# Extra TensorE products without a reader at three kinds of waits in a decoder layer

## The reference

```python
x = x + _L0_attn_ref(_layernorm(x))
x = x + _L0_xattn_ref(_layernorm(x), ctx_512, Wq, Wkv_expand, Wout)
x = x + _L0_ffn_ref(_layernorm(x), w_gate, w_up, w_down)
```

## Time and profile before

| | us |
|---|---|
| three runs, median (lowest to highest) | 1776.98 (1774.51 to 1780.01) |
| the profiled execution's own time | 1770.3 |
| its span, first to last instruction | 1767.3 |
| PE busy | 1404.7 (79%) |
| DVE busy | 1141.0 (65%) |
| ACT busy | 857.7 (49%) |
| POOL busy | 547.8 (31%) |
| mean granted clock of TensorE | 0.926 |

### The profile page before, as it was taken

How to read it: one execution, slowest core, us unless ns; L and a number is a source line. 1 busy time by engine, 2 the same in 40 slices (tenths; PEclk the granted TensorE clock), 3 DMA queues, 4 the chain that set the end, 5 groups by cost and what they waited for, 6 DMA issues and landing times.

```text
span 1767.3 us, 30712 instructions
## 1 busy us (share of the span) xinstructions
PE 1404.7 (79%) x11035; PEld 815.5 (46%) x11104; DVE 1141.0 (65%) x2475; ACT 857.7 (49%) x2098; POOL 547.8 (31%) x494
## 2 busy tenths in 40 slices
PE   1224898889988898779988899779988899779977
PEld 0113554445544554445544554445544554445533
DVE  8993355864578455864578455864578456864576
ACT  2442364445634564455634564455635564455622
POOL 5872000650046200640046101640046101640045
PEclk9999899898989899998989899998989899998998
DMA  5311000000010000010010000010010001000001
GB/s 184 107 54 37 1 1 23 9 17 9 1 25 13 19 1 25 7 25 1 2 24 13 19 1 25 7 25 1 1 25 13 19 2 25 7 19 1 1 0 24
DMA packets 25283, 36.04 MB, mean 20 GB/s; under 512 B 2480, under 2 KB 10672, under 8 KB 25136
## 3 DMA queue, kind: packets, MB, share of 16 engines
q1 hardware_dynamic: 25136, 34.09, 7.3%
HBM read 25.69 MB, written 8.39 MB: 19 GB/s over the span
## 4 chain that ended last, share of the span: by engine, by line
PE 45%; DVE 25%; ACT 10%; issue 9%; POOL 2%; DMA 0%; SPq 0%; ACTq 0%; DVEq 0%; POOLq 0%
PE psum L1092 10%; PE psum L526 8%; PE psum L1109 7%; PE psum L1130 5%; DVE top L807 4%; DVE inter L833 3%; PE psum L1146 3%; PE psum L1169 3%; PE psum L1095 3%; PE psum L1191 2%; ACT silu L990 2%; DVE nmx L757 2%; DVE q L803 2%; DVE xn L508 2%; PE psum L1118 1%
## 5 line engine op out<-in xcount | busy, mean ns | idle before, releaser
L757 DVE TENSOR_REDUCE nmx<-psum 128x2 f32<-128x256 f32 (+3 forms) x256 | 211.0, 824 | 209.4 <-PE psum L1095 207.4
L503 POOL TENSOR_TENSOR rstd<-var_eps,minus_half 128x1 f32<-128x1 f32 x96 | 59.9, 624 | 867.3 <-DVE var_eps L497 867.1
L952 ACT ACTIVATE p<-psum,nmx 128x384 f32<-128x384 f32 (+3 forms) x512 | 265.9, 527 | 65.3 <-DVE nmx L757 58.8
L1092 PE MATMUL psum<-k_f,q_f 32*128 32x128 f32 (+3 forms) x1024 | 226.7, 520 | 11.7 <-ACT q_f L932 5.9
L770 DVE COPY pt<-psum 128x128 f32<-128x128 f32 (+3 forms) x256 | 124.6, 487 | 159.9 <-PE psum L1109 159.4
L1109 PE MATMUL psum<-ident,p 128*128 128x128 f32 x1280 | 205.2, 288 | 19.7 <-ACT pt L976 16.5
L691 POOL TENSOR_TENSOR inter<-inter,rscale 128x512 f32<-128x512 f32 x128 | 141.5, 1105 | 213.4 <-DVE rscale L841 212.8
L1191 PE MATMUL psum<-wd_sb,iq_t 128*128 128x512 bf16 x503 | 146.2, 416 | 46.2 <-DVE x_res L850 27.1
L976 ACT COPY pt<-psum 128x128 f32<-128x128 f32 (+3 forms) x256 | 109.1, 426 | 149.4 <-PE psum L1109 148.0
L1109 PEld LDWEIGHTS psum<-ident,p 128*128 128x128 f32 x1280 | 143.0, 145 | 54.4 <-ACT pt L976 24.8
L1169 PE MATMUL psum<-wg_sb,xq_t 128*128 128x512 bf16 x452 | 132.8, 415 | 39.4 <-ACT xq_t L983 29.9
(11 more groups left out here) (102 smaller groups left out, 2389.8 us busy)
## 6 DMA issues: line engine op xcount, KB each, us to landing
x_in<-in_x_dram SPq DMA_DIRECT2D x32, 256.0 KB, 4.0
out_dram<-x_res SPq DMA_DIRECT2D x64, 128.0 KB, 2.4
w_raw<-in_w_gate_dram SPq DMA_DIRECT2D x16, 256.0 KB, 2.7
w_raw<-in_w_up_dram SPq DMA_DIRECT2D x16, 256.0 KB, 3.0
w_raw<-in_w_down_dram SPq DMA_DIRECT2D x16, 256.0 KB, 3.8
ctx_in<-in_ctx_t_dram SPq DMA_DIRECT2D x8, 256.0 KB, 2.9
wq_raw<-in_wq_t_dram SPq DMA_DIRECT2D x1, 1024.0 KB, 8.1
wo_sb<-in_wo_t_dram SPq DMA_DIRECT2D x1, 1024.0 KB, 10.0
```

The lines of the kernel that those rows point to most:

```text
L757: dve.tensor_reduce(nmx2[:, u % UNITS, 2 * pr:2 * pr + 2], where(("scores2", oc, qt, pr))[:, :, 0:(qt + 1) * P], AX_X, ALU.max, negate=Tru ...
L952: ins = act.activation(p2[:, (4 * u + hh) % P2_RING, 0:m], where(label)[:, hh % 2, 0:m], ACT.Exp, bias=nmx2[:, u % UNITS, hh:hh + 1], accu ...
L1092: pe.matmul(where(label)[:, j, 0:m], q_f[rows, oc % 2, qt * P:(qt + 1) * P], k_f[rows, oc % 2, 0:m], start=True, stop=False)
```

## The change

A helper `keep_busy` waits until a PSUM slot is free and then issues a number of products into it: the bf16 identity is the stationary operand, 512 columns of `wd_sb` are the moving one, and the result has no reader; the label's own products overwrite it. It is called at four places, of three kinds: three products before a batch's first scores and four behind them (in the slot of the first transposed probabilities), four before each tile's first gate product, between the tile's transposes and the wait for ACT's copy, and seven before a batch's first quantised transposes of the inner result. In `gate_up` the wait for the slot is put ahead of the wait for the copy of `xq_t`.

```diff
@@ -1048,6 +1048,12 @@
             @block.tensor
             def _(pe):
 
+                def keep_busy(label, times):
+
+                    until_free(pe, label)
+                    for _ in range(times):
+                        pe.matmul(where(label)[:, 0, :], ident_b[:], wd_sb[:, 0, :], start=True, stop=True)
+
                 def project_q(oc):
                     out_cols = slice(oc % OC * P, (oc % OC + 1) * P)
                     until_free(pe, ("q", oc))
@@ -1161,9 +1167,10 @@
                 def gate_up(i):
                     t, m = divmod(i, 4)
                     label = ("gateup", i)
+                    until_free(pe, label)
                     if m == 0:
+                        keep_busy(label, 4)
                         until_freed(pe, ("xqT", t))
-                    until_free(pe, label)
                     for j, w in enumerate((wg_sb, wu_sb)):
                         for c in range(C):
                             last = pe.matmul(where(label)[:, j, :], xq_t[:, t % 2, c * P:(c + 1) * P],
@@ -1209,8 +1216,10 @@
                 for b in range(B):
 
                     first, end = b * UNITS, (b + 1) * UNITS
+                    keep_busy(("scores2", *units[first], 0), 3)
                     for pr in range(2):
                         score2(first, pr)
+                    keep_busy(("probsT2", *units[first], 0), 4)
                     for u in range(first, end):
                         oc, qt = units[u]
                         more = oc % OC + 1 < OC
@@ -1243,6 +1252,8 @@
                             gate_up(b * CHUNKS + i)
                         if INTER_LAG < i <= CHUNKS + INTER_LAG:
                             down(b * CHUNKS + i - INTER_LAG - 1)
+                        if i == INTER_LAG:
+                            keep_busy(("interT", b * CHUNKS), 7)
                         if INTER_LAG <= i < CHUNKS + INTER_LAG:
                             turn_inter(b * CHUNKS + i - INTER_LAG)
                         if b + 1 < B:
```

## The result

The changed kernel takes 1722.83 us (median of 4 runs, 1719.87 to 1724.87), the kernel before 1775.74 (4 runs, 1770.95 to 1780.01). The ratio is 0.970, with a 95% interval from 0.968 to 0.973. That is faster by 53 us; 1740 was forecast, with 1729 to 1750 around it. The profiled execution took 1723.65 us, with a span of 1721.9; between the two spans there are 45.4 us.

A forecast was written before the change was run, and what follows sets the result against it. TensorE at half clock behind each batch's first scores was taken as the bound. 35.0 there + 1.9 feed-forward - 0.4 added products = 36.5 us off 1770.3, 2.1%, giving 1740 us from the 1776.98 median; range 1729 to 1750, outer 1722 to 1760.

The forecast's parts named there:

- The mechanism: Behind each batch's first scores: short pauses precede the clock's fall; filling them holds 1.00 and gives 35.0 us.
- the marks: Each unit's closing transpose on L1118; foretold 4.8 and 7.95 us behind the first mark and the one after it.
- Rival 1: First scores: high clock holds in some batches only, each fall returns 4.5 us; four of eight give 1757; chance 0.12.
- Rival 2: Clock falls for another reason than the pauses, or products don't count; 0 to 3 us added, 1777 to 1780; chance 0.06.
- The first mark: First scores: stretch from 405.35 to the first unit's closing transpose, 1.77 us low, 0.97 high; 0.80 us gained a batch.
- the sum for the first groups: First group of heads, all eight batches: 8 x (0.80 + 2.16) + 2.27 + 4 x 1.4 + 3 x 1.15 = 35.0 us gained.
- The feed-forward part: First quantised transposes to next first scores: 4.7 us gained, 2.8 us paid back by low-level products, net 1.9 us.
- the 4.7 us expected for the fall: First quantised transposes: the fall goes, giving 0.9 us in batches 1, 3, 5 and about 1 in 0 and 7.
- One sign of being right: Feed-forward part: its length stays within 1 us of 92.5.
- The loss at the gate: First gate product: four products at low level take 1.71 us against at most 1.1; about 0.7 us late a tile.
- rival 3: Slower: low-level products on the path, at the gate 0.7 us a tile; 1783 to 1799, 1791 taken; chance 0.06.
- The lower bound of 1722: Whole kernel: range's low end, if scores give 40 and feed-forward 6 us and timed runs hold more low stretches.

The follow-up runs named there:

- the first experiment: Changed kernel with only the products before and behind the first scores (3 + 4), none at the gate or quantised transposes: 1726.60 us, ratio 0.975.

## Why the prediction was right, and where its sum was short

**The mechanism was right at the first scores.** The granted clock behind them is 1.00 in all eight batches; the marks are 4.78 and 7.96 us apart as foretold. The 64-column products and the seven placed early speak for work in the pauses behind the scores and against the rivals. Over all traces, 55 of the 56 first groups with four or eight full products behind the scores stay high throughout, and none of the 40 with no product there does. Of the seven added products only the four matter; the three before the scores, which the prediction counted as part of the remedy, do nothing. Rival 1 (it holds in some batches only) didn't happen in the changed kernel; with the same products at the scores it did in one batch of the first experiment. Rival 2 falls: the pauses are all shorter than a microsecond, and filling one of 0.73 us in each batch is worth some 40 us in all. The section of the Trainium skill (TensorE: Matmul & The Clock Gate, "Why this matters for your kernels") names only a long idle gap; taken as the only way to the low level, this does not agree with the traces here, and the measurement decides.

**The first mark was mis-sized.** "What lies between the fall and 405.35 I count at nothing" was wrong. Between the transpose at 403.67 and the scores at 405.35 stand three products of `project_k`; that takes 1.68 us before, and 396.78 - 395.83 = 0.95 after. The row that the sum left out, in the kernel before:

```profile
403.80 1.63 PE L526 MATMUL psum<-ctx_hl,wkv_hl 128*128 128x512 f32 x3
```

From the first scores to the first mark it was 8.44 us and is 6.98, 1.46 us a batch less and not 0.80: 5.3 us in eight batches. With this term the sum for the first groups is 40.3, and 40.2 was measured.

**The feed-forward part gave 4.7 us, not 1.9, and not where the sum had it.** The fall behind the first quantised transposes did go, and with it 1.4 us of the step from the first to the second tile in batches 1, 3 and 5. But these parts are no shorter: 93.4 us each before, 93.8, 93.2 and 93.2 after. From the fourth tile's transposes to the next scores they take 35.9 us instead of 34.8, with a low stretch of 6.8 us near the end (in batch 1 from 569.8) where 3.4 us were low before. Batch 1, first the kernel before, then the changed one, with the transposes of the second and fourth tile (the first tile's and the next scores of the kernel before are in the earlier trace rows, of the changed one in its rows here):

```profile
519.46 0.61 PE L1157 MATMUL psum<-ident_b,xq 128*128 128x128 bf16 x4
562.48 0.40 PE L1157 MATMUL psum<-ident_b,xq 128*128 128x128 bf16 x4 [0.73 <-ACT iq_t L998]
```

```profile
490.98 0.38 PE L1163 MATMUL psum<-ident_b,xq 128*128 128x128 bf16 x4 [0.20 <-POOL xq L691]
505.14 0.40 PE L1163 MATMUL psum<-ident_b,xq 128*128 128x128 bf16 x4
548.90 0.61 PE L1163 MATMUL psum<-ident_b,xq 128*128 128x128 bf16 x4
549.73 1.49 PE L1055 MATMUL psum<-wd_sb,ident_b 128*128 128x512 bf16 x3 [0.22 <-issue]
551.01 1.81 PE L1176 MATMUL psum<-wg_sb,xq_t 128*128 128x512 bf16 x4
584.81 0.49 PE L1098 MATMUL psum<-k_f,q_f 32*128 32x128 f32 x4
```

The 4.7 us came from batch 0 (1.4), the last batch (2.4), and batches 2, 4 and 6 (1.1 together), for which the sum had nothing; batches 1, 3 and 5 together lost 0.1, where 0.9 each was expected. That this adds up to the 4.7 us expected for the fall is luck. One sign of being right, a part within 1 us of 92.5, was missed in batch 1.

The loss at the gate was met three times: in the fourth tile of batches 1, 3 and 5 the four products ran at the low level, and the first gate product came 1.91 to 2.11 us behind the tile's first transpose. In the first experiment, without products at the gate, it is 1.38 us at that level:

```profile
546.80 0.61 PE L1163 MATMUL psum<-ident_b,xq 128*128 128x128 bf16 x4
548.18 1.86 PE L1175 MATMUL psum<-wg_sb,xq_t 128*128 128x512 bf16 x4 [0.77 <-ACT xq_t L983]
```

So the price of 0.5 to 0.7 us at the gate, rival 3's, is real (0.7 was taken), but it isn't seen further on: from the fourth tile's transposes to the next scores, these parts take the same 35.9 us in the run without the gate's products.

**The pauses at the high level hold the products**, as costed: the four behind the first scores add some 0.08 us a batch (2.14 us between the two scores, 2.06 in the run with all seven before them), where 0.05 was taken. Where they don't fit, each costs its 0.216 us (0.86 for four).

**The start and the base.** 0.7 us lies in front of the first scores of batch 0. That moment differs between executions of one kernel (199.0 and 194.5 us in the two traces of the kernel before), so I don't put it down to the change. The sum is then 40.2 + 4.7 + 0.7 = 45.6, within 0.2 of the 45.4 us between the spans, against 36.5 forecast. The lower bound of 1722 stood for 40 us at the scores and 6 in the feed-forward part: the first is what came, the second came near by luck. The medians differ by 52.9. Of that the two profiled executions' own times show 46.7; the other 6.2 are the distance of these executions from their medians, nearly all of it that of the kernel before (1770.3 against 1775.74). In the later sessions its median was 1772.5 to 1774.6, which leaves a gain of 50 to 52. The second trace of the kernel before shows that its first groups alone vary by 4 us with the length of the low stretches. What else makes the longer executions longer is open: both that were profiled are among the short ones.

## What to carry to other kernels

A stretch where TensorE waits a little and often can cost far more behind it than in it: here pauses of 0.7 us, which are nothing by themselves, put the next 14 to 17 us of TensorE-bound work at half speed. Compare the same instructions at both levels in one trace to price it, count every dense run in the stretch, and then fill a pause shortly ahead of the fall (here one that ends 3 us before it), with no more than it holds; here the same products two microseconds earlier did nothing. Where another engine sets the pace, the low level costs little (here 13.7 us of it some 0.6 us) and filling is not worth much; here a later low stretch got longer as an earlier one went.

## What was not expected of the hardware

- Place beats amount: four products (0.87 us) behind the first scores keep the level in eight of eight batches of their own run, seven before them (1.5 us) in none.
- Once low, the clock stayed low for 13.6 us in batch 1 of the kernel before while TensorE's busy time is all of the stretch by modelled ends. It rose during the dense run of the query projection, twelve products of 512 columns:

```profile
415.43 3.90 PE L526 MATMUL psum<-x_t,wq_hl 128*128 128x512 f32 x12
...
405.00:417.20 12.20, 12.20 (x57) 6.01 (x57) 4.21 (x7) 5.83 (x19) 0.00 (x0) 0.50 0.00 0
417.40:424.00 6.60, 5.68 (x46) 3.80 (x48) 2.89 (x6) 2.99 (x8) 0.00 (x0) 1.00 0.00 0
```

- Falls also come at places where the first trace has none: with the feed-forward products alone, a third group of heads in two batches (23.1 us instead of 21.6) and the output part in one (15.45 us from its last mark to the next transposes, instead of 13.75), and in the second trace of the unchanged kernel a third group in one batch.
